# Mixture of experts: weighing, cleaning and scattering beside the products; two projections moved inside the scan

## The chip, the cores and the metric

One core of one Trainium2 chip runs the whole program in one launch. The metric is device time in microseconds (us) of one execution, from launch to end. The profiled execution also has a span, from its first to its last instruction on the engines: PE (TensorE, matrix products), DVE (VectorE), ACT (ScalarE), POOL (GpSimd) and SP (SyncE, which only issues transfers here).

## The reference, cut to what matters

Four layers run on an image of 2 x 256 channels x 48 x 48, which is M = 4608 tokens of 256 channels. The change touches the first layer's selective scan and the last layer's capacity-limited mixture of experts.

```python
# layer 0: projection, short convolution, gates, then a scan forward and one backward
xz = h @ in_proj_w.T ; xi, z = split(xz)
y_f = _mamba_branch(xi, z, ...)              # conv -> silu -> proj -> dt, B, C
y_b = _mamba_branch(xi[:, ::-1], z[:, ::-1], ...)[:, ::-1]
    # step: h = exp(d_t*A) * h + (d_t*u_t) * B_t ;  y = sum(h * C_t) ;  return y * silu(z)

# layer 3: 8 experts, capacity C = ceil(1.25*T/E); T is M here, so C = 720
probs = softmax(x @ gate_w + gate_b) ; idx = argmax(probs) ; prb = probs[idx]
pos = running count of idx - 1 ; kept = pos < C
buf = zeros((E, C, D)).at[idx, where(kept, pos, C)].set(x, mode='drop')
ybuf = relu(buf @ w1 + b1) @ w2 + b2
y_tok = ybuf[idx, min(pos, C-1)] * (prb * kept)
y = nan_to_num(y_tok, nan=0.0, posinf=10000.0, neginf=-10000.0)
t = t + y
```

## The kernel before

**The scan (`mamba_chunks`).** The tokens of an image are cut into 5 chunks (`MC`) of at most 461; with two images and two directions there are 20 chunks (`NCH`), g = 0 to 19: five forward and five reverse of image 0, then of image 1. Each chunk has 64 steps (`STEPS`), one for each pair of a state (16) and a channel block (4). A step is an exponential on ACT (L785, `DA`), a product on POOL (L930, `DBU`), the scan itself (L974) and a product with C (L985, `G`) on DVE, and a matmul with the identity on PE that sums G in PSUM (L613). The four engines run hand in hand through semaphores. All other work of a chunk is put into fixed steps `s` of the loop by written-out conditions, on each engine: the input projection of the chunk after next (`xi(g + 2, j)` on PE, L492, and `take_xi` on ACT, L669), the gate `z` of a reverse chunk (L552, `take_z` L736, `exp_z` L741), the convolution (`conv`, L514), the step size (`dt_part`, `floor_rest` L728, POOL's `log_rest` L889). The projection and the gate share PSUM banks 0 and 1, the convolution has 2 and 3. Chunk g = 8 is called `LATE`: the chunk after next is the first forward chunk of image 1, and its four projections stand at steps 62 and 63 on PE. ACT takes two of them at step 63 and two at steps 0 and 1 of chunk 9.

**Clearing the buffer (`gated_experts`, layer 2).** While PE works on the last two of nine pieces of this layer, SP writes zeros in nine transfers of 640 KB to `buf_dram`, the experts' input buffer (L2898), and waits for them before the block ends.

**Routing (`route_images`).** Tokens are normalized in 12 tiles, transposed to rows (`XT`), and gated; for each of 4 groups of 9 x 128 tokens DVE works out expert, position and probability (`shift`, `choose`, `place`). `place` leaves three things: `SI`, the row in the buffer (or one out of bounds for a token over capacity), `GI`, the row to gather from later, and `WT`, probability times kept. POOL scatters 36 x 128 rows of 1 KB with indirect transfers (L3277). SP loads the gate's weights and the first two experts.

**The experts (`experts`).** For each of 8 experts, 720 rows (6 tiles of `RT` = 120) are loaded (`XR`, L3536), transposed on PE for the next expert (L3555, copied by DVE at L3610), and multiplied: 16 groups for the hidden layer (L3571, ReLU on ACT at L3595), then 6 tiles of 8 matmuls (L3579). DVE adds the bias of each tile (L3622) and ACT issues its store to `y_dram` (L3599). PE may run at most two tiles ahead of that addition.

**The last stage (`combine`).** It starts when all of `experts` is done, its stores included. For 9 groups of 4 x 128 tokens: POOL gathers rows of `y_dram` by `GI` (L3654), ACT weighs them by `WT` (L3669) and takes absolute values (L3673), DVE clears a tile, compares with the largest finite number, clamps and copies by predicate (L3684 to L3693), PE puts the residual `X` into PSUM (L3702) and adds the transposed rows (L3707), ACT copies the sum back to `X` (L3663), and SP stores it to the output (L3719). Between stages a block of SP clears the semaphores (`fresh`).

Of the kernel before, what the change touches and what calls it, by code (L numbers as in the profile page):

```python
# [24 lines left out]
NB = 2  # L25
# [288 lines left out]
def mamba_chunks(nc, ctx, k, A, w):  # L314
# [36 lines left out]

    used = sems(nc, ctx, "da_done", "dbu_done", "h_done", "hc_done", "g_done", "acc_done", "y_taken",
# [15 lines left out]
    def xi_at(g):  # L368
        if g == LATE:
            return 62, 62, 63, 63  # L370
        return (55, 56, 59, 60) if is_rev(g - 1) else (47, 48, 52, 53)

    def xi_taken(g):
        return (58, 59, 61, 62) if is_rev(g - 1) else (52, 53, 57, 58)


    with nc.Block() as block:
# [101 lines left out]
        def _(pe):  # L479
            def xi(h, j):  # L480
                b, at, n = tokens(h)
                if j < 2 and h:
# [8 lines left out]
                for i in range(KC):  # L491
                    mm = pe.matmul(PS[:, j % 2, HALO - halo:HALO + n], w.w_in[:, i, j * P:(j + 1) * P],  # L492
# [84 lines left out]
            def first(g, p):  # L577
# [10 lines left out]
                else:  # L588
                    if g + 1 < NCH:
# [19 lines left out]
            for S in range(STEPS * NCH):  # L609
# [31 lines left out]
                if is_rev(h):  # L641
                    if s == 52:
                        z(h, 0)
                    elif s == 55:
                        z(h, 1)
                    elif s == 58:
                        z(h, 2)
                    elif s == 60:
                        z(h, 3)
# [11 lines left out]
        def _(act):  # L661
            def take_xi(h, j):
# [6 lines left out]
                act.activation(XI[:, j, HALO - halo:HALO + n], PS[:, j % 2, HALO - halo:HALO + n], ACT.Copy).then_inc(xi_in, 1)  # L669
# [108 lines left out]
            for S in range(STEPS * NCH):  # L778
# [13 lines left out]
                if h < NCH:  # L792
# [28 lines left out]
                    elif s == 56:  # L821
# [7 lines left out]
                if is_rev(h):  # L829
                    if s == 57:  # L830
                        take_z(h, 0)
                    elif s == 58:
                        exp_z(h, 0)
                    elif s == 59:
                        take_z(h, 1)
                    elif s == 60:
                        exp_z(h, 1)
                    elif s == 61:
                        take_z(h, 2)
                    elif s == 62:  # L840
                        exp_z(h, 2)
                    elif s == 63:
                        take_z(h, 3)
# [10 lines left out]
                if is_fwd(g + 2) and g != LATE and s in xi_taken(g):  # L854
                    take_xi(g + 2, xi_taken(g).index(s))
                if g == LATE and s == 63:
                    take_xi(g + 2, 0)
                    take_xi(g + 2, 1)
                if g == LATE + 1:
                    if s == 0:  # L860
                        take_xi(g + 1, 2)
                    elif s == 1:
                        take_xi(g + 1, 3)
# [1988 lines left out]
def gated_experts(nc, k, A, g):  # L2852

    with ExitStack() as ctx:
# [19 lines left out]
        with nc.Block() as block:  # L2874
            @block.sync
            def _(sp):
# [23 lines left out]
                sp.wait_ge(k.buf_clear, 16 * ZN)  # L2900
# [309 lines left out]
ZW = NE * CAP * C // (P * ZN)  # L3210


def route_images(nc, k, A, st):
# [9 lines left out]
    with ExitStack() as ctx:  # L3223
# [6 lines left out]
        XT = sb("XT5", [P, TM, C])  # L3230
# [652 lines left out]
```

## Time and profile before

| What | Value |
|---|---|
| Runs of the kernel | 5589.03, 5555.76, 5595.31 us; median 5589.03 |
| Profiled execution, own time | 5566.04 us |
| Its span | 5564.3 us |
| PE busy over the span | 4733.6 us, 85% |
| DVE busy over the span | 3402.2 us, 61% |
| Mean granted clock of PE | 0.947 of full |

The profiled execution's time is 1.7 us over its span, and 23.0 us under the median; the three runs lie 39.6 us apart. Times in rows are microseconds from the start of the span, durations of one instruction in groups are nanoseconds. In brackets stands how long the engine was idle before an instruction, and what ended that. "SPq" and "ACTq" are those engines' instruction queues, which issue transfers.

### The profile page before, as it was taken

To read this page: it belongs to the slowest core of one execution; us is meant where nothing else is said; L and a number is where in the kernel's file an instruction comes from. 1 tells how busy PE (TensorE), PEld (TensorE's weight loads), DVE (VectorE), ACT (ScalarE), POOL (GpSimd) and SP (SyncE) were. 2 spreads that over 40 slices of the span, in tenths; PEclk is the share of its full clock that TensorE was granted. 3 is DMA by queue.
4 is the path that set the end of the run, shared out by engine and by line. 5 is a ranking of instruction groups with operands and counts; after the bars stand their busy time and mean duration, and the time that the engine had idled before them with its cause. 6 is when DMAs were issued, how large, how long until landed. Compare 5 with 4: busy or idle time off the path is not lost. (4 is left out here: it accounts for less than half of the span.)

```text
span 5564.3 us, 51138 instructions
## 1 busy us (share of the span) xinstructions
PE 4733.6 (85%) x14958; PEld 2627.4 (47%) x14959; DVE 3402.2 (61%) x4897; ACT 2102.2 (38%) x3413; POOL 2312.8 (42%) x2102
## 2 busy tenths in 40 slices
PE   5787789888878888699899899596999999995997
PEld 3333333333323333355455655473555555554775
DVE  2999999999999999679387365373232101002104
ACT  2666665666656666232232222121222222121223
POOL 2888898888889888302111100470000000003002
PEclk8999999999999999999999899797999999995998
DMA  2434433433444443100100001110111000000323
GB/s 88 151 111 147 137 127 120 134 120 117 129 144 131 127 137 106 65 31 0 55 30 15 31 4 42 22 20 14 59 39 56 1 0 2 0 33 17 86 85 79
DMA packets 221927, 390.74 MB, mean 70 GB/s; under 512 B 35071, under 2 KB 205988, under 8 KB 216828
## 3 DMA queue, kind: packets, MB, share of 16 engines
q1 hardware_dynamic: 207660, 374.28, 21.0%
q0 software_dynamic: 7552, 7.81, 0.9%
q10 hardware_dynamic: 6480, 5.90, 0.4%
q8 instruction: 101, 1.65, 0.1%
q14 instruction: 134, 1.10, 0.1%
HBM read 337.06 MB, written 53.42 MB: 70 GB/s over the span
## 5 line engine op out<-in xcount | busy, mean ns | idle before, releaser
L930 POOL TENSOR_TENSOR DBU<-DU,BB 128x461 f32<-128x461 f32 (+1 forms) x1280 | 1371.9, 1086 | 305.9 <-DVE PS L974 294.4
L613 PE MATMUL PS<-G,ident 128*128 128x461 f32 (+1 forms) x2560 | 1144.4, 573 | 389.6 <-DVE G L985 387.9
L974 DVE TENSOR_TENSOR_SCAN PS<-PS,HC,DBU 128x461 f32<-128x461 f32 (+1 forms) x1024 | 1149.7, 1167 | 13.7 <-ACT PS L785 12.3
L785 ACT ACTIVATE PS<-DT,alog 128x461 f32<-128x461 f32 (+1 forms) x1280 | 825.3, 645 | 725.6 <-DVE PS L974 724.9
L613 PEld LDWEIGHTS PS<-G,ident 128*128 128x128 f32 x2560 | 453.7, 191 | 1043.3 <-DVE G L985 832.0
L985 DVE TENSOR_TENSOR G<-PS,CB 128x461 f32<-128x461 f32 (+1 forms) x1280 | 786.0, 624 | 4.4 <-PE PS L613 4.4
L3067 DVE TENSOR_TENSOR X<-X,PS 128x768 f32 x12 | 11.4, 954 | 553.3 <-PE PS L3034 553.3
L3023 PE MATMUL PS<-QT,N 128*128 x864 | 310.2, 486 | 4.7 <-ACTq L3040 4.7
L3034 PE MATMUL PS<-AT,XT 128*128 128x384 f32 x864 | 310.5, 487 | 0.0
L974 DVE TENSOR_TENSOR_SCAN PS<-PS,DBU 128x461 f32<-128x461 f32 (+1 forms) x256 | 272.0, 1107 | 60.1 <-POOL DBU L930 56.7
L1363 POOL TENSOR_TENSOR X<-X,FF x12 | 41.8, 3484 | 637.2 <-ACT EV L1358 637.2
L3098 POOL TENSOR_TENSOR xs<-X 128x384 f32 x12 | 11.8, 992 | 700.1 <-issue 700.1
L1039 PE MATMUL PS<-TT,w_fc 128*128 x768 | 280.8, 494 | 12.2 <-ACTq L1063 12.2
L1049 PE MATMUL PS<-H,w_fc 128*128 128x384 f32 x768 | 275.3, 486 | 0.0
L3056 ACT ACTIVATE AT<-PS 128x384 f32<-128x384 f32 x216 | 105.3, 490 | 416.8 <-PE PS L3023 416.8
L514 PE MATMUL PS<-XI,cdiag 128*128 128x461 f32 (+1 forms) x640 | 260.0, 549 | 0.6 <-ACT XI L669 0.6
L2961 DVE TENSOR_TENSOR Hg<-Hg,GB 128x384 f32<-128x384 f32 x144 | 80.4, 558 | 258.5 <-ACT Hg L2943 247.9
L1077 ACT ACTIVATE H<-PS,b_fc 128x384 f32<-128x384 f32 x192 | 111.0, 580 | 325.5 <-PE PS L1039 325.4
L3023 PEld LDWEIGHTS PS<-QT,N 128*128 128x128 f32 x864 | 164.0, 190 | 119.2 <-issue 5.2
L3034 PEld LDWEIGHTS PS<-AT,XT 128*128 128x128 f32 x864 | 163.7, 190 | 115.5 <-issue 2.6
L2916 PE MATMUL PS<-NN,w1g 128*128 128x384 f32 x576 | 209.0, 491 | 4.4 <-PEq L57 4.4
L2930 PE MATMUL PS<-Hg,w2g 128*128 128x384 f32 x576 | 207.3, 488 | 0.0
(444 smaller groups left out, 7392.1 us busy)
## 6 DMA issues: line engine op xcount, KB each, us to landing
BB<-proj_dram SPq DMA_DIRECT2D x256, 461.0 KB, 4.0
CB<-proj_dram SPq DMA_DIRECT2D x64, 922.0 KB, 6.1
BB<-proj_dram SPq DMA_DIRECT2D x64, 460.0 KB, 4.7
ew<-in_l_w SPq DMA_DIRECT2D x16, 1024.0 KB, 6.8
CB<-proj_dram SPq DMA_DIRECT2D x16, 920.0 KB, 6.3
w_fc<-in_l_w_fc SPq DMA_DIRECT2D x4, 2048.0 KB, 11.6
XI<-xi_dram SPq DMA_DIRECT2D x8, 928.0 KB, 5.0
xi_dram<-XI SPq DMA_DIRECT2D x8, 922.0 KB, 6.3
```

Of the source, the lines that this page charges most:

```text
L514: mm = pe.matmul(PS[:, 2 + j % 2, :wide(h)], w.cdiag[:, j, t, :], XI[:, j, at:at + wide(h)], start=(t == 0), stop=(t == TAP - 1))
L613: pe.matmul(PS[:, j, :wide(g)], k.ident[:], G[:, S % 4, :wide(g)], start=False, stop=(n == DS - 1))\
L785: act.activation(DA(S), DT[:, j, :wide(g)], ACT.Exp, scale=w.alog[:, chunk(g)[1], j, n:n + 1]).then_inc(da_done, 1)
L930: pool.tensor_tensor(DBU[:, S % 4, :wide(g)], DU[:, j, :wide(g)], BB[:, 2 * u + n % 2, :wide(g)], ALU.mult).then_inc(dbu_done, 1)
L974: dve.tensor_tensor_scan(flow(HS(S), g), flow(DA(S), g), flow(DBU[:, S % 4, :wide(g)], g), start, ALU.mult, ALU.add).then_inc(h_done, 1)
L985: dve.tensor_tensor(G[:, S % 4, :wide(g)], HS(S), CB[:, n, :wide(g)], ALU.mult).then_inc(g_done, 1)
L1039: mm = pe.matmul(k.PS[:, s % 3, :T], w1(j, s), src(j, c), start=(j == 0), stop=(j == KC - 1))
L1049: mm = pe.matmul(k.PS[:, 4 + 2 * u + o, :T], w2(m, o), H[:, m, :], start=(m == 0), stop=(m == NM - 1))
L2916: mm = pe.matmul(k.PS[:, s % 3, :T], w1[:, j, s * P:(s + 1) * P], g.NN[:, j, c * T:(c + 1) * T], start=(j == 0), stop=(j == KC - 1))
L2930: mm = pe.matmul(k.PS[:, 4 + 2 * u + o, :T], w2[:, m, o * P:(o + 1) * P], H[:, m, :], start=False, stop=(m == NM - 1))
L3023: mm = pe.matmul(k.PS[:, s % NA, :T], k.N[:, j, s * P:(s + 1) * P], QT[:, j, bass.ds(c * T, T)], start=(j == 0), stop=(j == KC - 1))
L3034: mm = pe.matmul(k.PS[:, 4 + 2 * u + o, :T], XT[:, m, o * P:(o + 1) * P], AT[:, m % NA, :], start=(m == 0), stop=(m == LT - 1))
```

## The change

In the scan: the four projections of the `LATE` chunk move to steps 26, 27, 29 and 30 on PE and 30 to 33 on ACT, in PSUM banks 2 and 3; the gate's products move from steps 52, 55, 58, 60 to 51, 54, 56, 58 and ACT's part of them one step earlier; `floor_rest` of the next chunk moves from step 56 to 55. In the mixture: a row in `buf_dram` gets two more columns (its token number plus one, and its probability), so 1032 bytes; `y_dram` becomes a buffer of token rows and is zeroed too; experts weigh, clean and scatter their results themselves; `combine` loads plain rows.

```diff
+    def xi_bank(h, j):
+        return j % 2 + (2 if h == LATE + 2 else 0)
     def xi_at(g):
         if g == LATE:
-            return 62, 62, 63, 63
+            return 26, 27, 29, 30
     def xi_taken(g):
+        if g == LATE:
+            return 30, 31, 32, 33
@@ xi on PE
+                if j < 2 and h == LATE + 2:
+                    pe.wait_ge(cv_exp, JD * (h - 1) + 3 + j)
+                    if j == 0:
+                        pe.wait_ge(y_taken, 2 * (h - 2))
@@ first(g, 1) on PE, at step 31
+                    if g == LATE:
+                        pe.wait_ge(xi_in, JD * (fwd_before(g + 2) + 1))
@@ z on PE: 52, 55, 58, 60 -> 51, 54, 56, 58 ; on ACT each one step earlier
-                    elif s == 56:
+                    elif s == 55:
                         floor_rest(h, 0)
@@ gated_experts, SP
+                for n in range(ZY):
+                    sp.dma_start(k.y_dram...[n], zero[:, 0:M * C // (P * ZY)]).then_inc(k.buf_clear, 16)
+                sp.wait_ge(k.buf_clear, 16 * (ZN + ZY))
@@ route_images
+                sp.dma_start(tok[:], A["c_tok"]).then_inc(tok_in, 16)
...
-                    dve.tensor_tensor(st.WT[:, at], prb, kept, ALU.mult)
+                    dve.tensor_copy(XT[:, at, C + 1], prb)
-                    dve.tensor_scalar(total, pos, float(CAP - 1), None, ALU.min)
-                    dve.tensor_tensor(st.GI[:, at], total, base, ALU.add)
...
+                dve.wait_ge(tok_in, 16)
+                dve.tensor_copy(XT[:, :, C], tok[:])
@@ experts, ACT (after the ReLUs of expert e)
+                act.wait_ge(slots_done, e + 1)
                 for t in range(NR):
-                    act.wait_ge(y_done, NR * e + t + 1)
-                    act.dma_start(k.y_dram[...], YB[:, u, t, :]).then_inc(y_sent[u], 16)
+                    n = NR * e + t
+                    act.wait_ge(y_done, n + 1)
+                    act.activation(YB[:, n % 2, :], YB[:, n % 2, :], ACT.Copy, scale=WT[:, e, t:t + 1])
+                    if n >= 2:
+                        act.wait_ge(y_clean, n - 1)
+                    act.drain()
+                    act.activation(AB[:, n % 2, :], YB[:, n % 2, :], ACT.Abs).then_inc(y_weighed, 1)
@@ experts, POOL
+                    pool.wait_ge(y_clean, NR * e + t + 1)
+                    pool.indirect_dma_start(out=k.y_dram, out_offset=...SI[:, e, t:t + 1]...,
+                        in_=OK[:, e % 2, t, :], bounds_check=M - 1, ...).then_inc(y_sent[e % 2], 16)
@@ experts, DVE
+            def slots(e):      # weight, and token number minus one (or out of bounds)
+                held = XR[:, e % 2, :, C]
+                dve.tensor_copy(WT[:, e, :], XR[:, e % 2, :, C + 1])
+                dve.tensor_scalar(AT[:, e, :], held, 0.5, NOWHERE, ALU.is_lt, ALU.mult)
+                dve.drain()
+                dve.scalar_tensor_tensor(SI[:, e, :], held, -1.0, AT[:, e, :], ALU.add, ALU.add)...
+            def clean(n):      # as combine did, on 120 x 256
+                dve.memset(ok, 0.0)
+                dve.wait_ge(y_weighed, n + 1)
+                ... 2 compares, clamp, drain, copy_predicated, drain, copy_predicated -> y_clean
                 for t in range(NR):
                     dve.tensor_tensor(YB[:, n % 2, :], k.PS[0:RT, 6 + t % 2, :C], b2[0:RT, u, :], ALU.add)
                     if e + 1 < NE:
                         take(e + 1, t)
+                        if t == NR - 1:
+                            slots(e + 1)
+                    if n >= 1:
+                        if t == 1 and e >= 2:
+                            dve.wait_ge(y_sent[u], 16 * NR * (e // 2))
+                        clean(n - 1)
+            clean(NR * NE - 1)
@@ combine, SP (POOL's, DVE's and ACT's weighing parts are gone)
+                def load(n):
+                    if n >= DEEP:                       # DEEP = 4
+                        sp.wait_ge(yt_ready, n - DEEP + 1)
+                    sp.dma_start(YG[:, n % DEEP, :, :], k.y_dram[n * GN:(n + 1) * GN, :]...)
+                for n in range(DEEP):
+                    load(n)
                 for n in range(NG):
+                    if n + DEEP < NG:
+                        load(n + DEEP)
                     sp.wait_ge(yt_added, n + 1)
                     ... store to out ...
@@ combine, PE
-                    pe.wait_ge(y_clean, n + 1)
+                    pe.wait_ge(yg_in[n % DEEP], 16 * (n // DEEP + 1))
```

## Rows read from the trace of the kernel before

**Rows 1.** Groups by line, DVE, to 2100 us: shapes, count; busy, mean; idle.
```profile
L974 DVE TENSOR_TENSOR_SCAN PS<-PS,HC,DBU 128x461 f32<-128x461 f32 (+1 forms) x912 | 1023.9, 1167 | 12.2 <-ACT PS L785 10.9 <-POOL DBU L930 1.3
```
**Rows 2.** Timeline, DVE: start, duration, instruction, idle before it.
```profile
676.36 1.12 DVE L974 TENSOR_TENSOR_SCAN PS<-PS,DBU 128x460 f32<-128x460 f32 x1 [0.34 <-ACT PS L785]
...
1111.91 1.19 DVE L974 TENSOR_TENSOR_SCAN PS<-PS,HC,DBU 128x461 f32<-128x461 f32 x1 [4.75 <-ACT PS L785]
1114.23 1.18 DVE L974 TENSOR_TENSOR_SCAN PS<-PS,HC,DBU 128x461 f32<-128x461 f32 x1 [1.14 <-ACT PS L785]
...
2182.68 1.19 DVE L974 TENSOR_TENSOR_SCAN PS<-PS,HC,DBU 128x461 f32<-128x461 f32 x1 [0.35 <-ACT PS L785]
```
**Rows 3.** Timeline, ACT, at the border of chunks 8 and 9.
```profile
1109.24 0.56 ACT L669 ACTIVATE XI<-PS 128x461 f32<-128x461 f32 x1 [2.30 <-PE PS L492]
```
**Rows 4.** Timeline, POOL, then ACT, in an ordinary chunk.
```profile
341.90 1.18 POOL L889 TENSOR_TENSOR V<-V,LN 128x461 f32<-128x461 f32 x1
...
344.64 0.96 ACT L728 ACTIVATE V<-V 128x922 f32<-128x922 f32 x1
```
**Rows 5.** Windows: length, busy (PE, PEld, DVE, ACT, POOL), clock, DMA share, GB/s.
```profile
4230.00:4240.00 10.00, 10.00 (x32) 5.89 (x31) 2.23 (x4) 2.32 (x4) 0.00 (x0) 1.00 0.87 356
...
4300.00:4310.00 10.00, 5.46 (x17) 2.86 (x16) 1.80 (x3) 1.86 (x2) 0.00 (x0) 1.00 0.09 26
```
**Rows 6.** Start of routing: timeline; DMA issues (KB, us to landing).
```profile
4980.29 0.68 SPq L3264 DMA_DIRECT2D key<-in_c_key  x1
...
4981.69 0.95 DVE L3459 TENSOR_TENSOR N<-X,PS 128x768 f32<-128x768 f32 x1 [2.44 <-PE PS L3314]
...
tri<-in_c_tri SPq DMA_DIRECT2D x1, 64.0 KB, 2.1
```
**Rows 7.** Timeline, PE, one tile of the experts' second product.
```profile
5441.31 3.62 PE L3579 MATMUL PS<-ew,HE 128*120 128x256 f32 x16
```
**Rows 8.** Groups by line, from 4900 us: weighing and cleaning in combine.
```profile
L3669 ACT ACTIVATE YG<-YG,WT 128x256 f32<-128x256 f32 x36 | 15.3, 497 | 40.5 <-DMA YG<-y_dram,GI 40.4
...
L3691 DVE COPY_PREDICATED OK<-MK,YG 128x1024 f32<-128x1024 int32 x9 | 12.0, 1334 | 0.7
...
L3684 DVE MEMSET OK<- 128x1024 f32 x9 | 8.2, 912 | 6.3 <-PEq L57 3.6 <-issue 2.7
...
L3688 DVE TENSOR_SCALAR MK<-AB 128x1024 int32<-128x1024 f32 x9 | 6.2, 684 | 0.0
```
**Rows 9.** Timeline: from routing to experts, then from experts to combine.
```profile
5137.66 0.97 POOL L3277 DMA_INDIRECT buf_dram<-XT,SI  x1 [0.30 <-issue]
5144.57 10.24 SPq L3536 DMA_DIRECT2D XR<-buf_dram  x3
...
5485.26 0.42 DVE L3622 TENSOR_TENSOR YB<-PS,eb 120x256 f32<-120x256 f32 x1 [3.03 <-PE PS L3579]
5488.98 0.50 PEld L3702 LDWEIGHTS PS<-X,ident 128*128 128x128 f32 x2 [4.17 <-issue]
```
**Rows 10.** Timeline, combine: PE in groups 0 and 4, last copy of ACT.
```profile
5504.20 3.78 PE L3707 MATMUL PS<-ident,OK 128*128 128x128 f32 x16 [11.43 <-DVE OK L3693]
...
5531.00 2.05 PE L3707 MATMUL PS<-ident,OK 128*128 128x128 f32 x16 [1.41 <-issue]
...
5532.89 1.88 PE L3702 MATMUL PS<-X,ident 128*128 128x512 f32 x4
...
5559.56 1.02 ACT L3663 ACTIVATE X<-PS 128x1024 f32<-128x1024 f32 x1 [6.28 <-PE PS L3707]
```
**Rows 11.** DMA queues, 5489 to 5564.3 us: packets, MB, share of 16 engines.
```profile
q0 software_dynamic: 1728, 4.72, 37.6%
q1 hardware_dynamic: 2720, 4.72, 16.8%
```
**Rows 12.** DMA queue, 5142 to 5156 us; then windows, all of combine.
```profile
q1 hardware_dynamic: 1537, 1.54, 57.1%
...
5489.00:5564.30 75.30, 41.18 (x180) 26.91 (x180) 49.56 (x54) 33.73 (x54) 39.94 (x36) 0.82 0.55 126
```

More of the change, by code:

```diff
@@ L3209 @@
 ZN = 9
-ZW = NE * CAP * C // (P * ZN)
+CX = C + 2
+ZW = NE * CAP * CX // (P * ZN)
+ZY = 9
+NOWHERE = 8192.0
 def route_images(nc, k, A, st):
@@ L3229, in route_images @@
         rstd = sb("rstd", [P, DEEP, TT])
-        XT = sb("XT5", [P, TM, C])
+        XT = sb("XT5", [P, TM, CX])
+        tok = sb("tok", [P, TM])
         LG = sb("LG", [P, QT_, NE])
@@ L3498, in capacity_mixture @@
             experts(nc, own, k, A, st)
-        combine(nc, k, st, out)
+        combine(nc, k, out)
 def load_expert(sp, A, st, e):
@@ L3631, with combine @@
 NG = TM // GT
-def combine(nc, k, st, out):
+def combine(nc, k, out):
     GN = GT * P
+    DEEP = 4
     with ExitStack() as ctx:
@@ new lines, in combine, with _ @@
+        YG = sb("YG", [P, DEEP, GT, C])
+        used = sems(nc, ctx, "yg_in0", "yg_in1", "yg_in2", "yg_in3", "yt_ready", "yt_added", "stored")
+        yg_in, (yt_ready, yt_added, stored) = used[:DEEP], used[DEEP:]
+        with nc.Block() as block:
+            @block.sync
+            def _(sp):
+                def load(n):
+                    if n >= DEEP:
+                        sp.wait_ge(yt_ready, n - DEEP + 1)
+                    sp.dma_start(YG[:, n % DEEP, :, :], k.y_dram[n * GN:(n + 1) * GN, :].rearrange("(t p) c -> p t c", p=P))\
+                      .then_inc(yg_in[n % DEEP], 16)
+                count = 0
+                for n in range(DEEP):
+                    load(n)
+                for n in range(NG):
+                    if n + DEEP < NG:
+                        load(n + DEEP)
+                    sp.wait_ge(yt_added, n + 1)
+                    for b in range(NB):
+                        lo, hi = max(n * GN, b * L), min((n + 1) * GN, (b + 1) * L)
+                        if lo < hi:
+                            sp.dma_start(out[b].rearrange("(k p) n -> p k n", p=P)[:, :, lo - b * L:hi - b * L],
+                                         k.X[:, :, lo:hi]).then_inc(stored, 16)
+                            count += 16
+                sp.wait_ge(stored, count)
@@ L3753, in build @@
         k.early_dram = nc.dram_tensor("early_dram", [EARLY * E2, P, KC, T], F32, kind="Internal").ap()
[L3754 to L3755 removed]
+        k.buf_dram = nc.dram_tensor("buf_dram", [NE * CAP, CX], F32, kind="Internal").ap()
+        k.y_dram = nc.dram_tensor("y_dram", [M, C], F32, kind="Internal").ap()
         k.row_sent = ctx.enter_context(nc.semaphore("row_sent"))
[L3758 removed]
         k.zeroed = ctx.enter_context(nc.semaphore("zeroed"))
```

168 lines of the change are left out of this document (65 added, 103 removed).

## The prediction

> **What bounds the kernel now.** I read the page first: the chain that ended last names only lines of the last stage and shares of a tenth of a per cent, so no one line bounds the kernel. The stages stand one behind another, and each has to be read by itself. Then the groups by line and the timeline of VectorE for the scan, the timelines of the last 600 us, and the DMA queues of the last stage.
>
> The scan is bound by VectorE. In the first 2100 us its 912 scans of the main form took 1023.9 us and waited for 12.2 us in all [rows 1]. The timeline shows where it did wait: 4.75 and 1.14 us at the border of chunks 8 and 9, for ScalarE's exponential, and eleven waits of 0.30 to 0.35 us, 3.70 us in all, at the borders ahead of reverse chunks, of which the first and the last are shown [rows 2]. The reader is to see at 1109.24 what ScalarE did instead of the exponential: it stood 2.30 us waiting for the projection that PE issues at step 62, and took its result [rows 3].
>
> The experts are bound by PE: a tile of the second product takes 3.62 us without a gap [rows 7]. The last stage is bound by no engine. It lasts 75.3 us, in which PE is busy for 41.2, DVE for 49.6 and POOL for 39.9 us, and the transfers run at 126 GB/s [rows 12]. It is a chain per group: gather, weigh, clean, transpose.
>
> **The change part by part.**
>
> *Scan.* The four projections leave the border of chunks 8 and 9, so 4.75 + 1.14 = 5.89 us go. At steps 26 to 33 they cost the same 4 x 0.56 us on ScalarE [rows 3] and the same products on PE, beside a VectorE that needs some 3.3 us for two steps. ScalarE has 2 x 0.65 us of exponentials in that time and 2 x 0.56 us of copies, so it has cover; PE has two accumulations and two projections, about 1.1 + 2.2 us, and then four products of `first` at step 31. That is full, and DVE may wait for an accumulation once. I take 0.6 us for it; the bounds are 0 and the 5.89 us of the old place. Gate products a step or two earlier: nothing is queued behind them that was not before, and ScalarE no longer has two of the gate's instructions after the last exponential of a chunk. I take all 3.70 us; the bounds are 0 and 3.70. `floor_rest` a step earlier waits for POOL's second `log_rest`, which ends at 341.90 + 1.18 = 343.08; the floor itself started at 344.64 and needs 0.96 us [rows 4]. From 343.1 to 344.1 it fits ahead of the next exponential; behind it are queued the exponentials, and DVE is next to wait if it doesn't fit. Nothing taken. Scan: -5.9 - 3.7 + 0.6 = **-9.0 us**.
>
> *Zeroing `y_dram`.* Nine more transfers, 4.72 MB, on SP's queue behind the first nine and ahead of nothing. At the 356 GB/s of the first ones they take 13.3 us, to some 4254, while PE works in that block to about 4305 [rows 5]. Cost nothing; uncovered it would be 13.3 us.
>
> *Routing.* `tok` is SP's fifth transfer. It is issued at 4980.29 + 0.68 = 4980.97 and lands 2.1 us later by the row of `tri`; 0.2 us of copy follow, so DVE reaches its first subtraction at 4983.3 in place of 4981.69 [rows 6]. Queued behind the wait is all of DVE's normalizing, and PE, ACT and POOL wait for that: **+1.6 us**, bounds 0 (absorbed later) and 2.5. The two experts' loads behind it on SP start 0.5 us later and are needed 160 us on. `place` loses two instructions of nine elements: nothing. The scatter of 1032 bytes for 1024 and the load of the first experts' rows: 1.54 MB took 57.1% of 14 us, 8.0 us, a rate of 193 GB/s [rows 12]; 0.8% more of 720 KB is 0.03 us. Later loads have two experts' time. Nothing taken; the bounds are 0 and, if an odd row costs double, 3.8 us.
>
> The Trainium skill ("DMA: Bandwidth & Descriptors", section "How a descriptor splits into AXI transactions") speaks against these rows: a transfer that doesn't start on a multiple of 256 bytes still begins at the boundary below, and the bytes in front cost time. Counted by its table a row of 1032 bytes has 33 to 39 beats where an aligned one of 1024 has 32, so the first load would take up to a fifth, about 0.8 us, longer, and the sum would be -27.2 for -28.0. No transfer here shows it.
>
> *Experts.* DVE gets a cleaning per tile. Its six instructions on 1024 elements cost 0.912 + 3 x 0.684 (the clamp taken as a compare) + 2 x 1.334 = 5.63 us; a quarter of that is 1.41, with some 0.5 us for fixed parts and drains 1.9 us [rows 8]. With the 0.42 us of bias and about 0.4 of copy a tile costs DVE 2.7 us, under PE's 3.62 [rows 7], and PE may be two tiles ahead. ScalarE's weighing is 0.50 us and its absolute value less than that, where it only issued stores before; they stand ahead of the next expert's ReLUs, which have four PSUM banks of cover. POOL issues 48 scatters of 0.97 us, and did nothing before. So 48 tiles cost nothing, as long as DVE's tile stays under 3.62 us.
>
> *From experts to combine.* Before: 5485.26 (the last bias) to 5488.98, 3.7 us. After: 0.42 of bias, the cleaning of tile 46, which DVE does first (1.9), that of tile 47 (1.9), 0.1 of handing over, POOL's 0.97, and then what routing needs from the end of its last scatter to the next stage's first transfer, 5144.57 - 5138.63 = 5.94 us [rows 9], less 1.0 because here no scatters are backed up. That is 10.2 us: **+6.5**. Bounds: with the way from the last bias to combine as before, less the bias (3.3 us), 8.6 us, so +4.9; with the full 5.94, +7.5.
>
> *Combine.* POOL's 36 gathers, 3 x 9 instructions of weighing and so on leave. What is left per group is PE's 2.05 + 1.88 = 3.93 us at the full clock, ScalarE's 1.02 beside it, and transfers. The first group: a transfer lands 2.1 us after issue [rows 6], plus 0.52 MB at 193 GB/s, 2.7 us [rows 12]: 4.8. Its transposes come after a pause and take 3.78 us as group 0 did at half the clock [rows 10]; 1.5 us more for what follows before it rises. Then 8 x 3.93 = 31.4, the last copy and store 4.74 (5559.56 to 5564.3, [rows 10]). Transfers: the loads 4.72 / 0.193 = 24.5 us, the stores 16.8% of 75.3 = 12.7 us [rows 11], together 37.2 us against PE's 35.4. With both that near, I add 2 us for friction. 4.8 + 3.8 + 1.5 + 31.4 + 2 + 4.7 = 48.2 us for 75.3: **-27.1**. Bounds: 44.7 without clock and friction, and 75 if transfers keep the 126 GB/s of before.
>
> Sum: -9.0 + 1.6 + 6.5 - 27.1 = **-28.0 us**. Against the profiled execution's own 5566.0 us that is 5538. That execution is 23 us under the median of 5589; neither is more right than the other, so I apply the sum to the middle of both, 5577.5: **5550 us**, 0.5 to 0.7% less than before.
>
> **Rivals.**
>
> 1. *Combine is bound by transfers.* For it: small rows, loads and stores on one queue of SP, and gathers that took 37.6% of the engines for the same bytes that need 16.8% as stores [rows 11]. Against: rows of experts came at 193 GB/s [rows 12]. If it stays at 126 GB/s, the stage lasts 75 us and the sum is -9.0 + 1.6 + 6.5 = -0.9: 5577 us.
>
> 2. *The scan's wait only moves.* PE's step 31 has to wait for four copies at steps 30 to 33, and what went at the border comes back there, 5.9 us, and the small waits stay, 3.7. For it: the count of PE above is full. Against: one border, no repetition. -18.4: 5559 us.
>
> 3. *Slower: DVE becomes the experts' bound.* The place is the wait of PE for the bias two tiles back, in each expert's second product. It decides from a DVE tile of 3.62 us, a cleaning of 2.8. Were cleaning's cost fixed rather than by width, 5.6 us of cleaning give a tile of 6.4 us; PE would lose 2.8 us on some 40 tiles (two of each eight experts' tiles are cover, and the rest of 48 waits), 112 us with nothing given back: 5660 us. For it: many short instructions with drains. Against: weighing 256 elements took 0.50 us, so width does count [rows 8]. From a cleaning of 3.4 us (28 / 48 more) the whole change would be a loss.
>
> 4. *Nothing at the borders, all in combine.* Both gains come as forecast but the gate's small waits have another cause: -24.3, 5553 us; it differs too little from the forecast to be told in time.
>
> **How the numbers follow.** Forecast 0.64, rival 1 0.14, rival 2 0.10, rival 3 0.03, rival 4 0.09. The forecast's own terms reach from -35 (bounds on the good side: scan -9.6, routing 0, entry 4.9, combine 44.7) to about -18. Applied to 5566 for the low end and to 5589 for the high end that is 5531 to 5571; the base is not known better than those two, and with rival 2 and part of rival 1 the range is 5528 to 5578. About 1% (56 us) is what a measurement of this kernel tells from no change. The sum is half of that; it gets there only where the good bounds meet runs as far apart as the 39.6 us shown: 0.12 faster. Slower needs rival 3: 0.03. Same: 0.85.
>
> **What would show it.** In the scan: VectorE has no wait of over 1 us at the border of chunks 8 and 9, and steps 30 to 34 of chunk 8 show one under 1 us. In routing the first subtraction starts some 1.6 us later after the stage's start. In the experts PE runs without gaps and DVE's cleaning instructions sum to 1.4 to 1.9 us a tile. From the last bias to combine 9 to 11 us; the stage itself 45 to 52 us with PE's groups about 4 us apart, and a DMA share near 0.8. It is wrong if groups come 6 us or more apart, or if PE waits for DVE in the experts.

## The result, and the profile after

| | before | after |
|---|---|---|
| Median of 20 runs | 5591.1 us | 5550.8 us |
| Lowest to highest | 5555.3 to 5625.9 | 5532.2 to 5594.0 |
| Ratio, 95% interval | | 0.9939, 0.9919 to 0.9958 |
| Profiled execution, own time | 5566.0 us | 5545.6 us |
| Its span | 5564.3 us | 5543.8 us |

The change makes the kernel 0.6% faster, 34 us with an interval of 23 to 45. That is inside the range and in the class "within 1%" that the forecast gave.

I cut both spans into stages at the first transfer that SP issues in each. The scan ends with the transfers of the second layer's vectors.

| Stage | before | after | difference |
|---|---|---|---|
| First layer, scan included | 2306.8 | 2293.1 | -13.7 |
| Next four stages | 1252.4 | 1252.8 | +0.4 |
| Gathering by edge (layer 2) | 299.2 | 318.6 | +19.4 |
| Gating with the zeroing, sigmoid attention | 1120.6 | 1118.1 | -2.5 |
| Routing | 165.6 | 167.7 | +2.1 |
| Experts, to the last addition | 340.7 | 341.2 | +0.5 |
| Last addition to last stage | 3.7 | 12.8 | +9.1 |
| Last stage | 75.3 | 39.5 | -35.8 |

The spans differ by 20.5 us and the medians by 40. The stage in the third row, which the change does not touch, makes most of that difference; the experiments come back to it.

**Scan.** The group of VectorE to 2100 us, which answers to [rows 1]:

```profile
L978 DVE TENSOR_TENSOR_SCAN PS<-PS,HC,DBU 128x461 f32<-128x461 f32 (+1 forms) x918 | 1030.7, 1168 | 3.9 <-ACT PS L796 2.5 <-POOL DBU L934 1.3
```

The waits for the exponential fell from 10.9 to 2.5 us. On the new line numbers L978 is the scan, L796 the exponential and L989 the product with C. At the border of chunks 8 and 9 two scans now run as one entry without a bracket, where [rows 2] had 4.75 and 1.14 us of idle time. Timeline of VectorE there:

```profile
1108.76 0.63 DVE L989 TENSOR_TENSOR G<-PS,CB 128x461 f32<-128x461 f32 x1
1109.31 2.24 DVE L978 TENSOR_TENSOR_SCAN PS<-PS,HC,DBU 128x461 f32<-128x461 f32 x2
1111.46 0.62 DVE L989 TENSOR_TENSOR G<-PS,CB 128x461 f32<-128x461 f32 x1
```

The place to which the projections moved, ScalarE and then VectorE:

```profile
1048.66 0.55 ACT L680 ACTIVATE XI<-PS 128x461 f32<-128x461 f32 x1 [1.23 <-PE PS L501]
...
1051.75 0.56 ACT L680 ACTIVATE XI<-PS 128x461 f32<-128x461 f32 x1 [2.00 <-PE PS L501]
1052.20 0.64 ACT L796 ACTIVATE PS<-DT,alog 128x461 f32<-128x461 f32 x1
```
```profile
1052.88 1.18 DVE L978 TENSOR_TENSOR_SCAN PS<-PS,HC,DBU 128x461 f32<-128x461 f32 x1 [0.93 <-ACT PS L796]
```

This is the picture of [rows 3] again: ScalarE stands 2.00 us in line for a product of PE, and the exponential behind it comes late. VectorE pays 0.93 us where it paid 5.89.

**Routing.** SP, then VectorE, at the start of the stage:

```profile
4982.60 0.33 SPq L3272 DMA_DIRECT2D gate_w<-in_l_gate_w  x1
...
4984.66 0.43 SPq L3276 DMA_DIRECT2D tok<-in_c_tok  x1
```
```profile
4987.17 0.20 DVE L3462 COPY XT<-tok 128x36 f32<-128x36 f32 x1 [4.28 <-DMA tok<-in_c_tok]
4987.27 1.81 DVE L3471 TENSOR_TENSOR N<-X,PS 128x768 f32<-128x768 f32 x2
```

The first subtraction stands 4.67 us behind the stage's first transfer; before it was 2.73. VectorE is let go 2.5 us after the transfer's issue.

**Experts.** A tile of the second product still takes PE 3.62 us without a gap. VectorE's instructions of a cleaning, and what it waits for (groups, 5160 to 5490 us):

```profile
L3663 DVE COPY_PREDICATED OK<-MK,YB 120x256 f32<-120x256 int32 x46 | 20.6, 448 | 3.4
L3665 DVE COPY_PREDICATED OK<-MK,CL 120x256 f32<-120x256 int32 x46 | 20.6, 447 | 3.7 <-issue 0.4
L3677 DVE TENSOR_TENSOR YB<-PS,eb 120x256 f32<-120x256 f32 x47 | 19.9, 424 | 207.3 <-PE PS L3597 207.3
...
L3661 DVE TENSOR_SCALAR CL<-YB 120x256 f32<-120x256 f32 x46 | 13.2, 286 | 0.0
L3660 DVE TENSOR_SCALAR MK<-AB 120x256 int32<-120x256 f32 x46 | 12.9, 280 | 0.0
L3656 DVE MEMSET OK<- 120x256 f32 x46 | 12.5, 272 | 0.1
L3659 DVE TENSOR_SCALAR MK<-AB 120x256 int32<-120x256 f32 x46 | 10.8, 234 | 0.0
```

The six means sum to 1.97 us (the forecast had 1.9), and in each tile VectorE still waits 1.06 us for PE's product. A tile costs it 2.6 us.

**From experts to the last stage.** VectorE's last copy, POOL's last scatter, SP's first load, PE:

```profile
5495.33 0.44 DVE L3665 COPY_PREDICATED OK<-MK,CL 120x256 f32<-120x256 int32 x1
5496.61 1.00 POOL L3630 DMA_INDIRECT y_dram<-OK,SI  x1 [1.00 <-DVE OK L3665]
5504.29 6.71 SPq L3714 DMA_DIRECT2D YG<-y_dram  x5
5504.33 3.75 PE L3738 MATMUL PS<-X,ident 128*128 128x512 f32 x4 [12.90 <-PEq L57]
```

The last addition starts at 5491.47, so its two cleanings end 4.30 us later at 5495.77. POOL starts 0.84 us after that, and from the end of its scatter (5497.61) to the first load pass 6.68 us.

**Last stage.** Timeline of PE, two groups, which answer to the last of [rows 10]; then the window of the whole stage, as in [rows 12], and the queue:

```profile
5512.16 1.95 PE L3743 MATMUL PS<-ident,YG 128*128 128x128 f32 x16
5513.94 1.88 PE L3738 MATMUL PS<-X,ident 128*128 128x512 f32 x4
...
5515.66 1.95 PE L3743 MATMUL PS<-ident,YG 128*128 128x128 f32 x16
5517.45 1.88 PE L3738 MATMUL PS<-X,ident 128*128 128x512 f32 x4
```
```profile
5504.30:5543.80 39.50, 33.90 (x180) 23.47 (x180) 0.00 (x0) 9.21 (x9) 0.00 (x0) 0.93 0.70 240
```

PE has no bracket behind the first group: it waits for no transfer. Groups come 3.50 us apart, though the two durations sum to 3.83; the entries overlap (1.78 us from one to the next for a duration of 1.95). The starts say how fast PE goes, and the durations can't be added up. The stage moves its bytes at 240 GB/s, where it had 126.

### The profile page after: what moved, and what is told of

It reads as the page before. It is cut to its first block and busy times, and to the rows that moved or that the text cites. A ratio compares the mean times of both kernels' runs of the same rounds, so it can differ in the third digit from the quotient of the medians.

```text
span 5543.8 us, 51619 instructions
## 1 busy us (share of the span) xinstructions
PE 4723.3 (85%) x14958; PEld 2624.9 (47%) x14959; DVE 3434.4 (62%) x5148; ACT 2126.5 (38%) x3464; POOL 2317.8 (42%) x2114
## 5 line engine op out<-in xcount | busy, mean ns | idle before, releaser
L978 DVE TENSOR_TENSOR_SCAN PS<-PS,HC,DBU 128x461 f32<-128x461 f32 (+1 forms) x1024 | 1149.5, 1168 | 3.9 <-ACT PS L796 2.5
L796 ACT ACTIVATE PS<-DT,alog 128x461 f32<-128x461 f32 (+1 forms) x1280 | 825.1, 645 | 727.5 <-DVE PS L978 726.7
L989 DVE TENSOR_TENSOR G<-PS,CB 128x461 f32<-128x461 f32 (+1 forms) x1280 | 786.6, 625 | 3.4 <-PE PS L624 3.4
L978 DVE TENSOR_TENSOR_SCAN PS<-PS,DBU 128x461 f32<-128x461 f32 (+1 forms) x256 | 271.7, 1106 | 57.8 <-POOL DBU L934 55.7
```

What stands on the lines that cost most here:

```text
L796: act.activation(DA(S), DT[:, j, :wide(g)], ACT.Exp, scale=w.alog[:, chunk(g)[1], j, n:n + 1]).then_inc(da_done, 1)
L978: dve.tensor_tensor_scan(flow(HS(S), g), flow(DA(S), g), flow(DBU[:, S % 4, :wide(g)], g), start, ALU.mult, ALU.add).then_inc(h_done, 1)
L989: dve.tensor_tensor(G[:, S % 4, :wide(g)], HS(S), CB[:, n, :wide(g)], ALU.mult).then_inc(g_done, 1)
```

## The experiments

Time alone can't tell the parts apart: they are worth 0.2 to 0.6%, and the intervals are about 0.3% to each side. So each kernel was also profiled and read by its stages. For the scan I used one more reading: the time from the first product with C of one pair of steps to that of the next. It is 3.30 us where nothing is late. The pair that ends a chunk (steps 62 and 63) is called the border here. Experiments 5, 6, 8 and 12 are one execution each, read by the profile alone.

**1. The scan's part alone.** The scan's hunks of the change, and nothing of the mixture.

> Before with the scan's part of the change alone. The last gate_y transfer of the profile stood at 2306.8 us before and at 2293.1 after. Theory A (the two parts don't touch each other): it stands at 2293 +- 1 here, all later stages last as they did before, and the edge stage, if it is run-to-run, lasts anything from 299 to 319 us; time 14 us under before (ratio 0.9975). Theory B (code elsewhere shifts the scan, for instance by its semaphores or memory places): it stands 3 us or more away from 2293.

First layer 2293.8 us: theory A. Time: ratio 0.9987 (0.9957 to 1.0017), which settles nothing.

**2. The LATE move alone.**

```diff
-            return 62, 62, 63, 63
+            return 26, 27, 29, 30      # and 30..33 on ScalarE, banks 2 and 3
```

> Before with the move of the LATE chunk's four projections alone; gate products, their exponentials and floor_rest stay where they were. Theory A (the prediction's terms): the first layer ends 5.3 us earlier than before, at 2301.5, and the 8.4 us that are then left of 13.7 come from the gate and floor_rest. Theory B (moving LATE out of the border is worth more than its two waits, since instructions around it are stretched too): it ends at 2297 or earlier, and the other edit is worth 3.7 us or less. Time 5 us under before by A, 10 by B.

First layer 2303.9 us, ratio 1.0012 (0.9984 to 1.0039). Theory A is nearer, but the stage as a whole turned out to vary by itself (see 4), so the pairs decide:

| us | before | LATE alone | gate alone (5) | both (1) | after |
|---|---|---|---|---|---|
| border of chunks 4 and 5 | 4.03 | 4.03 | 3.17 | 3.17 | 3.17 |
| border of chunks 6 and 7 | 4.09 | 4.10 | 3.30 | 3.29 | 3.30 |
| border of chunks 8 and 9 | 9.39 | 4.10 | 9.41 | 3.29 | 3.29 |
| chunk 8, pair from step 30 | 3.30 | 4.34 | 3.30 | 4.34 | 4.33 |
| chunk 8, pairs from 32 and 38 | 6.60 | 6.98 | 6.60 | 6.97 | 6.97 |

The move is worth 5.29 us at the border and costs 1.4 us at its new place: 3.9 net. All 19 borders together held 12.95 us over 3.30 each before, 7.68 with LATE alone, and -0.46 with both. So the scan's edits are worth 13.4 us at the borders and cost 1.4 in chunk 8, 12.0 net. The first layer as a whole took 2306.8 to 2308.4 us in the three profiles with the scan as before, and 2291.2 to 2300.4 us in the nine with both edits: 11 us less in the mean, and the 13.7 of the first pair is at the good end.

**3. The mixture's part alone**, the other hunks.

> Before with the mixture's part alone. Theory A: first layer to 2306.8 as before; routing to experts 167.7 (+2.1); last bias to combine's first transfer 12.8 (+9.1); combine 39.5 (-35.8); sum -24 us, ratio 0.9957. Theory B (the 19.4 us that the edge stage took more after belong to the mixture's part, by new places of the buffers): the edge stage takes 318 us here and 299 in the kernels without it.

Ratio 0.9982 (0.9958 to 1.0007); theory A's 0.9957 lies just outside. First layer 2307.4 us, routing 169.3, experts with the last stage 393.1 against 419.7: by its stages, the gains and losses of the change are there without its other part. The edge stage took 331.3 us.

**4. The kernel before, once more.**

> The kernel before once more, unchanged. Theory A (the edge-gathering stage varies from run to run): it lasts something else than the 299.2 us of the first profile, by more than 5 us, while every other stage repeats within 1 us; ratio 1.000. Theory B (its 319 us after are due to the change): 299 +- 2 here, and in every kernel without the change's mixture part.

Ratio 1.000 (0.9972 to 1.0029). The edge stage took 321.5 us, and so theory A holds against the suspicion that 319 belonged to the change. In all 14 profiles of this study it took 290 to 349 us, with and without the mixture's part: 290.7, 298.5, 299.2, 306.0 and 321.5 in the five that have the mixture as before. Its "every other stage within 1 us" was too strict: one attention stage took 390 to 394 us, and the sigmoid attention 668 to 677. The stage ahead of it took either 94.3 to 94.8 us (nine profiles) or 118.3 (five), in kernels that had the same code there. Together the two took 394.0 us in the profile of before and 413.0 in that of after. Without them the spans are 5170.3 and 5130.9 us, 39.4 apart; in the repeats 5169.2 and 5141.9 (of after, below), 27.3 apart. The mean of the two, 33, is what the medians' ratio says. One group of the edge stage in the two profiles of before, first and repeated (last column idle time), and the longest of such waits, in experiment 9:

```profile
L2519 POOL DMA_INDIRECT RS<-src_dram,IX x64 | 79.5, 1242 | 48.6 <-DMA IX<-idx_dram 30.0 <-issue 18.6
```
```profile
L2519 POOL DMA_INDIRECT RS<-src_dram,IX x64 | 80.1, 1251 | 69.7 <-DMA IX<-idx_dram 51.7 <-issue 18.0
```
```profile
3695.77 0.33 SPq L2494 DMA_DIRECT2D IX<-idx_dram  x1
3699.31 1.70 POOL L2523 DMA_INDIRECT RS<-src_dram,IX  x1 [35.04 <-DMA IX<-idx_dram]
```

POOL's gathers last the same, and its waits for loads of indices (`IX`) grow by 21.7 us where the stage grows by 22.3. Over the 14 profiles these waits lie between 26.7 us (experiment 1, stage 298.5) and 84.0 (experiment 9, stage 348.7), so nearly all of the stage's spread is there. In the third fence POOL has waited 35 us for a load that SP issued only 3.5 us before: the load comes late because it is issued late. What SP stood waiting for was not followed.

**5. The gate's products and exponentials alone, one step earlier.**

```diff
-                    if s == 52: / 55 / 58 / 60          # z on PE
+                    if s == 51: / 54 / 56 / 58
-                    if s == 57: ... s == 63: take_z, exp_z
+                    if s == 56: ... s == 63: exp_z      # floor_rest stays at 56
```

> Before with the gate's products and exponentials alone moved one step earlier (as after); floor_rest and the LATE chunk's projections stay. Read from the start of the last product with C of one pair of steps to that of the next pair: before, the pair of steps 62 and 63 ahead of a reverse chunk lasted 4.03 to 4.11 us at eight borders and 9.39 at that of chunks 8 and 9, where others last 3.30. Theory A (ScalarE's take_z and exp_z both at step 63 hold up the next exponential): all eight are 3.2 to 3.3 here and chunk 8's is 8.6; the last gate_y comes 7.3 us earlier than before. Theory B (floor_rest a step earlier gives it): the eight stay at 4.1, no gain.

There are nine such borders, not eight, and all fell to 3.17 to 3.30 us. Theory A there; `floor_rest` has no part in it. At the border of chunks 8 and 9 theory A missed: it had 8.6 us and the pair stayed at 9.41. While `LATE`'s projections are in that border the gate's edit gives nothing there; with them gone it gives 0.81. The first layer took 2303.2 us, 3.6 less than before and not 7.3: pairs from steps 8 and 18 were longer here, 141.9 us in all for 136.7 (see the last section). The border of chunks 5 and 6, VectorE, before and with this edit:

```profile
779.52 0.63 DVE L985 TENSOR_TENSOR G<-PS,CB 128x460 f32<-128x460 f32 x1
780.50 1.19 DVE L974 TENSOR_TENSOR_SCAN PS<-PS,HC,DBU 128x461 f32<-128x461 f32 x1 [0.35 <-ACT PS L785]
781.92 1.18 DVE L974 TENSOR_TENSOR_SCAN PS<-PS,HC,DBU 128x461 f32<-128x461 f32 x1 [0.24 <-ACT PS L785]
783.01 0.62 DVE L985 TENSOR_TENSOR G<-PS,CB 128x461 f32<-128x461 f32 x1
```
```profile
779.00 0.63 DVE L986 TENSOR_TENSOR G<-PS,CB 128x460 f32<-128x460 f32 x1
779.54 2.24 DVE L975 TENSOR_TENSOR_SCAN PS<-PS,HC,DBU 128x461 f32<-128x461 f32 x2
781.68 0.63 DVE L986 TENSOR_TENSOR G<-PS,CB 128x461 f32<-128x461 f32 x1
```

From the last product before the border to the first behind it are 3.49 us and 2.68. Of the difference of 0.81 the brackets show 0.59; I had counted 0.35, since I listed waits from 0.30 us on. The other 0.22 is no wait in any view: two scans in a row take 2.24 us, and alone 1.19 and 1.18, with their starts apart.

**6. The way into routing and into the last stage.** Two edits to after:

```diff
+                sp.dma_start(tok[:], A["c_tok"]).then_inc(tok_in, 16)     # now first
                 sp.dma_start(gate_w[:], A["l3_gate_w"]).then_inc(gate_in, 16)
@@ combine, SP: the experts' semaphores, no longer in a block of their own
                 for n in range(DEEP):
                     load(n)
+                for s in old:
+                    sp.sem_clear(s)
```

> After, with two edits: the token numbers' transfer goes first in SP's queue of the routing stage, and combine's SP clears the experts' semaphores behind its first four loads, not in a block of its own ahead of them. Theory A (both were plainly on the path): the first subtraction comes 2.7 us after the stage's first transfer (4.7 in after), and from the end of the last scatter to combine's first load pass 4.5 us or less (6.7 in after). Theory B (those 6.7 us are the scatter's own way to completion): 6.2 us or more stay, and only routing gains.

The first subtraction came 2.85 us after the stage's first transfer (4.67 in after, 2.73 before): that wait was on the path and is gone by the order of one queue. The whole stage says the same: 165.6 to 167.0 us in the five profiles without these numbers, 167.5 to 170.1 in the seven where their transfer is fifth, 166.6 and 166.8 in the two where it is first. From the last scatter's end (5505.44) to the first load (5511.01) were 5.57 us: clearing 15 semaphores in a block of their own cost 1.1. Neither theory had it: theory A asked for 4.5 or less, theory B for 6.2 or more.

**7. The residual added by VectorE.**

```diff
-                    for i in range(KC):
-                        pe.matmul(k.PS[...], k.ident[:], k.X[:, i, n * GN:(n + 1) * GN], start=True, stop=False)
-                            mm = pe.matmul(..., YG[...], k.ident[:], start=False, ...)
+                            mm = pe.transpose(..., YG[...], k.ident[:])
-                    act.activation(k.X[...], k.PS[...], ACT.Copy)
+                    dve.tensor_tensor(x, x, k.PS[...], ALU.add)
```

> After, with the residual added by VectorE: PE only transposes (16 per group, 1.95 us), its four products of X per group (1.88 us) are gone, and VectorE adds the result in PSUM to X, some 1.2 us per group, in place of ScalarE's copy. Theory A (combine is bound by PE, transfers wait for it): groups come 1.9 to 2.6 us apart where they came 3.50, the rate rises over 300 GB/s, and the stage lasts 27 to 33 us instead of 39.5. Theory B (transfers bind at the 240 GB/s of after): groups stay 3.5 us apart and the stage lasts 37 us or more.

Ratio to before 0.9935 (0.9918 to 0.9951). The last stage fell from 39.5 to 30.0 us and its groups came 2.3 us apart in the mean: theory A. (The profile counts 8 transposes per group here.) Its window, and PE in its middle:

```profile
5486.90:5516.90 30.00, 13.68 (x72) 11.64 (x72) 10.82 (x9) 0.00 (x0) 0.00 (x0) 0.61 0.89 315
```
```profile
5500.26 1.07 PE L3740 MATMUL PS<-ident,YG 128*128 128x128 f32 x8 [2.09 <-DMA YG<-y_dram]
...
5502.99 1.94 PE L3740 MATMUL PS<-ident,YG 128*128 128x128 f32 x8 [1.67 <-DMA YG<-y_dram]
```

Now transfers bind: PE waits for a load ahead of each of these groups, the DMA share is 0.89, and the rate 315 GB/s. So the forecast's first rival is a real limit, at 315 and not at 126 GB/s, and 9.5 us below where the change stands.

**8. Half of the last stage's stores left out.**

```diff
-   sp.dma_start(out[b]...[:, :, lo - b * L:hi - b * L], k.X[:, :, lo:hi])
+   sp.dma_start(out[b]...[:, 0:1, lo - b * L:hi - b * L], k.X[:, 0:1, lo:hi])
```

> After, with half of combine's stores left out (the second 128 channels of the output aren't written). Theory A (PE-bound): groups stay 3.50 us apart, the stage shortens by 1 us or less, at its end. Theory B (transfers bind): 25% fewer bytes, groups come 2.7 to 3.0 us apart and the stage lasts some 34 us.

Groups stayed 3.50 us apart, the rate fell to 184 GB/s, and the stage lasted 38.7 us. Theory A, from the other side:

```profile
5539.56 1.95 PE L3743 MATMUL PS<-ident,YG 128*128 128x128 f32 x16
...
5543.06 1.95 PE L3743 MATMUL PS<-ident,YG 128*128 128x128 f32 x16
```

**9. One block, with 7 and the transfer of 6.**

```diff
-            return 26, 27, 29, 30
+            return 25, 26, 28, 29
@@ experts and combine in one block; POOL no longer waits for its scatters
+            for u in range(2):
+                sp.wait_ge(y_sent[u], 16 * NR * (NE // 2))
+            for n in range(DEEP):
+                load(n)
```

> After, with four edits: LATE's four products on PE one step earlier (25, 26, 28, 29); the token numbers' transfer first in its queue; the experts and the last stage in one block, where SP itself waits for the scatters and then loads; the residual added by VectorE. Scan: in chunk 8 the pairs of steps 30 to 38 were 1.4 us longer in after (one 4.34, one 3.39, one 3.58 for 3.30); if ScalarE waited there for PE's products (1.2 to 2.0 us before its copies), 0.5 us or less is left; if it is the count of PE's work, 1.4 stays. Entry: from the end of the last scatter to the first load were 6.7 us, of which the semaphores were 1.1. Theory A (the rest is block borders): 2.5 us or less here. Theory B (the rest is the scatter's own way until its semaphore counts): 4.5 us or more. Last stage: 30 us from the first load, as in the kernel with the addition on VectorE. Whole: 5516 us by A, 5518 by B where before has 5580.

In chunk 8 the pairs from steps 30, 32 and 38 are 3.30, 3.29 and 3.30 us: all 1.4 us are back. So it was the order in time of PE's product and ScalarE's copy, and not the count of PE's work. At the end of the experts:

```profile
5557.24 1.00 POOL L3666 DMA_INDIRECT y_dram<-OK,SI  x1 [1.00 <-DVE OK L3699]
5559.43 6.28 SPq L3571 DMA_DIRECT2D YG<-y_dram  x5
```

1.19 us from the end of the scatter to the first load: theory A. The way of the scatter to its semaphore is no more than that, and 5.5 of the 6.68 us come with the two blocks, the clearing between them and POOL's part in them (experiment 12 takes this apart). Ratio to before 0.9919 (0.9891 to 0.9947); the forecast, 5516 us where before has 5580, is 0.9885 and lies just outside. Routing took 166.8 us, and experts with the last stage 379.9; after, on the same chip, had 169.1 and 392.4. By these two it beats after by 15 us. The ratios alone, with 10 below, overlap.

**10. After, once more.**

> After once more, unchanged. Ratio to before 0.994 +- 0.002; the edge-gathering stage anywhere from 290 to 331 us, borders ahead of reverse chunks 3.3 us, from routing to experts 167 to 169 us, the last scatter's end to combine's first load 6.7, combine 39.5.

Ratio 0.9961 (0.9938 to 0.9984), a gain of 22 us where the first comparison had 34, with an interval that overlaps it. The edge stage took 332.5 us, just outside of what I had given. The first layer took 2300.4 us with all borders at 3.30 or under, 7.3 us more than in the first profile of the same kernel. The pairs say where: those from steps 8 and 18 sum to 142.7 us over the 20 chunks, against 136.0. The section on the hardware takes this up.

**11. Cleaning three times over.**

```diff
+                for _ in range(2):      # written out: compares, clamp, drain, copy, drain, copy, drain
```

> After, with the two comparisons, the clamp and the two copies of every cleaning done three times: VectorE's work per tile of the experts' second product goes from 2.58 us to some 6.1 us, where PE has a tile in 3.62. Theory A (the prediction's rival: from 3.62 on PE loses the difference on 40 tiles): 2.5 x 40 = 100 us. Theory B (the difference is lost only where the lag, 2.5 us more with each tile, passes the one tile of 3.62 us by which an addition is ahead of its need; VectorE catches up while PE works on the hidden layer): each expert loses some 3 to 5 us, 25 to 40 us in all. Beside it 7 us between the last addition and the last stage by both.

Ratio to before 1.0146 (1.0111 to 1.0181); experts and last stage took 502.9 us, 110 more than in after (393.0, mean of its two profiles). The number is near theory A's 100 and 7, but its mechanism isn't in the trace. PE over one expert, and ScalarE at its end:

```profile
5385.85 3.69 PE L3597 MATMUL PS<-ew,HE 128*120 128x256 f32 x16 [2.50 <-DVE YB L3692]
...
5392.16 3.69 PE L3597 MATMUL PS<-ew,HE 128*120 128x256 f32 x16 [2.42 <-DVE YB L3692]
...
5395.89 5.01 PE L3589 MATMUL PS<-XB,ew 128*128 128x360 f32 x16
5406.19 2.17 PE L3589 MATMUL PS<-XB,ew 128*128 128x360 f32 x3 [5.29 <-ACT HE L3613]
```
```profile
5404.69 0.51 ACT L3619 ACTIVATE YB<-YB,WT 120x256 f32<-120x256 f32 x1 [5.32 <-DVE YB L3692]
5405.27 0.42 ACT L3623 ACTIVATE AB<-YB 120x256 f32<-120x256 f32 x1
5405.60 1.90 ACT L3613 ACTIVATE HE<-PS,eb 128x360 f32<-128x360 f32 x4
```

A tile costs VectorE 6.3 us. Four tiles of an expert run without a wait, the fifth and sixth wait 2.50 and 2.42 us here, as theory B has it (33.5 us in 15 waits). But then PE waits once more, 5.3 us, for a ReLU: ScalarE stands in line for the last tile's addition and only then comes to the next expert's ReLUs (36.1 us in 7 waits). These pauses cost more than themselves:

```profile
5185.00:5625.00 440.00, 358.62 (x1376) 257.50 (x1376) 268.99 (x866) 113.48 (x224) 53.49 (x46) 0.93 0.16 47
```

The granted clock is 0.93 here and 1.00 in after over its experts. The hidden layer's products were busy for 175.4 us where after had 158.4, the second layer's for 177.6 and 172.8. Waits and clock are 91 us, the way into the last stage some 7; 12 us I can't place. Theory B left out ScalarE's wait and the clock.

**12. SP waits for the scatters, in blocks as after.**

```diff
-            for u in range(2):
-                pool.wait_ge(y_sent[u], 16 * NR * (NE // 2))      # now SP's, behind its last load
```

> After, with the experts' last wait, that for the scatters of the results, on SP in place of POOL; both blocks and the clearing of the semaphores stay. In one block, with SP waiting, the first load came 1.2 us after the end of the last scatter; in after 6.7, of which the clearing is 1.1. Open are 4.4 us. Theory A (POOL is late with its way out of its wait and the block): they shrink by 3 us or more, 3.7 or less from the last scatter's end to the first load. Theory B (the borders of the blocks cost them, whoever waits): 6.2 us or more stay.

5.33 us from the end of the last scatter (5524.51) to the first load (5529.84). 1.35 us were POOL's wait, fewer than A's three and more than B's half. With 1.2 of the scatter and 1.1 of clearing, some 3.0 us are left. They are not the price of a border as such: in the kernel before, the same borders and 12 clearings took 1.4 us from the landing of the last store (5487.58) to the next stage (5488.98), with POOL idle for long. What POOL does at the end of a block in which it has just issued an indirect transfer would be the next thing to look at; no run here shows it.

## Why the prediction was right, and where it was lucky

The forecast of 5550 us met 5550.8, and that is luck. The sum under it, -28.0 us, met -34 by the ratio of the first comparison, -22 by that of the second, and about -33 by stages without the two that vary. The base made up for the difference: I took the middle of the profiled execution and the median, 5577.5, and the median of 20 runs was 5591. What bounds each stage was right. Sizes were off, in both directions, and two of the signs that I had named were missed: from the last bias to combine 12.8 us for 9 to 11, and the last stage 39.5 us for 45 to 52. Part by part:

- **LATE.** -5.9 + 0.6 forecast; -5.3 + 1.4 measured. Rival 2 was right that a part of the wait moves, and wrong on where: it had PE wait at step 31 for ScalarE's copies, and what happened is that ScalarE waited up to 2.00 us for PE's products. It gave back 1.4 of 5.3, and experiment 9 takes those away too.
- **Small waits.** -3.7 forecast; -8.1 measured over ten borders (0.86 at two, 0.80 or 0.81 at eight). The step that failed is the count of "eleven waits of 0.30 to 0.35 us": the second wait of a border lay under my threshold, and a broken pair of scans costs 0.2 us beyond its idle time. Rival 4 (other cause) is false.
- **Zeroing.** 0 forecast. The stage with it lasted 391.8 us before and 392.2 after, and 390.6 to 392.3 in all 14 profiles: nothing that can be told from 0.
- **Routing.** +1.6 forecast, +1.9 measured at the first subtraction: the transfer needed 2.5 us from issue and not 2.1.
- **Rows of 1032 bytes.** From the first load's issue to PE's first transpose passed 6.50 to 7.00 us in the five profiles with 1024 bytes, and 6.19 to 6.48 in the nine with 1032. The rule that stood against the change in the Trainium skill ("DMA: Bandwidth & Descriptors", "How a descriptor splits into AXI transactions") would have made this longer, by an estimate from its table 0.5 us: with each row 8 bytes further from a multiple of 256 the rows have 33 to 40 beats, 36.5 in the mean, and not the 33 to 39 that I had counted. It doesn't show here.
- **Experts.** 0 forecast, +0.5 measured; the cleaning's 1.9 us was 1.97. Rival 3's price came near in experiment 11 for a reason that I hadn't given; its claim that 3.62 us per tile decides wasn't tried between 2.6 and 6.3.
- **Entry.** +6.5 forecast, +9.1 measured. The failed step is "5.94 us, less 1.0 because here no scatters are backed up": it was 6.68, and only 1.19 of it the scatter's own way; 1.1 were the clearing, 1.35 POOL's wait, and some 3.0 stay open. POOL's start came 0.84 us after the copy for the 0.1 that I took.
- **Last stage.** -27.1 forecast, -35.8 measured. The mis-sized term is "PE's 2.05 + 1.88 = 3.93 us": start to start it is 3.50, and eight groups make 3.4 us of that. The 1.5 us for the slow clock and the 2 for friction did not come, the first transposes took 2.12 us for 3.78, and the first load landed after 4.2 us for 4.8. Transfers were no limit at 240 GB/s; they become one at 315. The stage varies by itself: it took 72.0 to 76.5 us in the five profiles with the mixture as before.

## What to carry to other kernels

Time a step from start to start of the same instruction, and not by summed durations or idle times: durations of PE overlap by a tenth here, and idle columns left out a quarter of a stall. When work moves off a border, ask at its new place which engine will stand in line for it; PE's products put one step further ahead of ScalarE's copies cost nothing here. Where a block ends on an indirect transfer that POOL has just issued, the way into the next block cost 5.3 to 6.7 us here, and in one block with one wait 1.2; with POOL idle, two borders and the clearing cost 1.4.

## What the runs showed of the hardware that I had not expected

**The clock makes the scan's time vary.** At the start of a chunk PE stands empty for 2.5 us and soon has four products `dt` (L548), for which ScalarE and then VectorE wait. After in its two profiles, PE at the start of chunk 17:

```profile
1965.50 3.36 PE L624 MATMUL PS<-G,ident 128*128 128x461 f32 x4 [2.51 <-DVE G L989]
1968.79 1.91 PE L548 MATMUL PS<-PJ,w_dt 17*128 17x461 f32 x4
```
```profile
1968.61 2.52 PE L624 MATMUL PS<-G,ident 128*128 128x461 f32 x4 [2.51 <-DVE G L989]
1971.06 3.44 PE L548 MATMUL PS<-PJ,w_dt 17*128 17x461 f32 x4
```

The granted clock is 1.00 ahead of the pause in both. In the 6 us from PE's restart it is 0.72 in the first and 0.58 in the second. Then the first is back at 1.00, and the second has 0.50 from 1972 to 1978, the lower of the two levels (1.2 of 2.4 GHz). In the second ScalarE gets its product late, and VectorE loses 0.7 us in the pair from step 8. The pair from step 18 is 1.0 us longer, and there VectorE waits for PE. PE's sums right behind the four products take 7.58 us for 12 where the first profile has 3.37 for 8 and then 1.42 us of idle time; in the second PE goes on to the convolution's products without any. That it is behind from there on to step 18 is argued from these rows, not tried:

```profile
1974.42 7.58 PE L624 MATMUL PS<-G,ident 128*128 128x461 f32 x12
...
1996.03 0.64 DVE L989 TENSOR_TENSOR G<-PS,CB 128x461 f32<-128x461 f32 x1 [0.92 <-PE PS L624]
```

Which of the two happens differs from run to run of the same kernel. Over the 20 chunks the pairs from these two steps made 136.0 to 142.7 us in the ten profiles with the gate's edit, 140.7 in the mean, and 136.7 to 138.5 in the four without it. Whether that edit makes the slow case more frequent, and so gives back some of its own gain, is not shown: the eight longest sums come from other chips than experiments 2 to 4. The Trainium skill ("TensorE: Matmul & The Clock Gate", Part 1) says of the products at a kernel's start that how many of them run at the low clock differs between runs of one kernel. The two profiles show the same in the middle of this one, with 1.91 and 3.44 us for the same four products.

**The runs' spread has a place.** Two stages of layer 2 took 393 to 467 us together in profiles of kernels that all have the same code there. That is as much as the runs of before lie apart (5555.3 to 5625.9 us), and more than the whole effect of the change. Experiment 4 has the wait in which most of it lies.
